# Receiver one-hots 4 and 5 of each ring made on GpSimd instead of VectorE, in a six-convolution graph network on one core

## The reference

```python
edge_index = jnp.stack([src, dst])
h = jnp.maximum(_layernorm(x, axis=-1), 0.0)
x = x + _L0_gnn_ref(h, edge_index, L0_gnn_W_l, L0_gnn_b_l, L0_gnn_W_r)
...
# in each convolution, in one form or another:
summed = jax.ops.segment_sum(x[src], dst, num_segments=n)
deg = jax.ops.segment_sum(jnp.ones_like(src, dtype=x.dtype), dst, num_segments=n)
agg = summed / jnp.maximum(deg, 1.0)[:, None]
out = agg @ W_l.T + b_l + x @ W_r.T
```

## Time and profile before

| | us |
|---|---|
| median of 3 runs (650.18 to 650.49) | 650.31 |
| the profiled execution | 649.73 |
| its span | 647.9 |
| PE busy | 632.0 (98%) |
| DVE busy | 373.8 (58%) |
| ACT busy | 304.1 (47%) |
| POOL busy | 112.5 (17%) |

### The profile page before, as it was taken

How to read it: one execution, slowest core, us unless ns; L and a number is a source line. 1 busy time by engine, 2 the same in 40 slices (tenths; PEclk the granted TensorE clock), 3 DMA queues, 4 the chain that set the end, 5 groups by cost and what they waited for, 6 DMA issues and landing times.

```text
span 647.9 us, 10703 instructions
## 1 busy us (share of the span) xinstructions
PE 632.0 (98%) x3079; PEld 514.0 (79%) x3080; DVE 373.8 (58%) x863; ACT 304.1 (47%) x628; POOL 112.5 (17%) x104
## 2 busy tenths in 40 slices
PE   6989999999999999999999999999999999999997
PEld 4346777777888888888888888888888998899886
DVE  6998999766885333222333787444989730541222
ACT  4886886645334454321223342223678752555210
POOL 2000000000332300321410321430364070000000
PEclk9999999999999999999999999999999999999999
DMA  6311111228450202240201231211200000000102
GB/s 217 114 21 22 31 30 30 42 55 243 122 140 16 49 0 82 61 101 17 49 0 42 57 102 28 45 20 50 82 0 1 2 2 1 0 2 0 50 18 95
DMA packets 57953, 33.04 MB, mean 51 GB/s; under 512 B 45756, under 2 KB 49652, under 8 KB 57912
## 3 DMA queue, kind: packets, MB, share of 16 engines
q1 hardware_dynamic: 56632, 29.99, 18.0%
q10 hardware_dynamic: 1280, 2.56, 1.1%
HBM read 17.20 MB, written 4.20 MB: 33 GB/s over the span
## 4 chain that ended last, share of the span: by engine, by line
PE 91%; DVE 3%; issue 2%; DVEq 1%; DMA 1%; ACT 1%; ACTq 1%; SPq 0%
PE ps L1605 34%; PE ps L1698 27%; PE ps L1737 13%; PE ps L1763 8%; PE ps L1584 7%; DVE src_hot L1119 1%; DMA wstage<-in_L_gnn_W_l 1%; PE ps L1598 1%; PE ps L1546 1%; DVE p_lo L1373 0%; DVE stats L1091 0%; DVEq L1119 0%; DVE dst_hot L1117 0%; DVE own L1333 0%; ACTq L374 0%
## 5 line engine op out<-in xcount | busy, mean ns | idle before, releaser
L1698 PE MATMUL ps<-p_hi,cstage 128*128 128x512 f32 x400 | 156.0, 390 | 0.5 <-ACT cstage L750 0.5
L1698 PE MATMUL ps<-p_lo,cstage 128*128 128x512 f32 x400 | 155.7, 389 | 0.0
L1605 PE MATMUL ps<-w_hi,hT_hi 128*128 128x512 f32 x320 | 126.2, 394 | 0.5 <-issue 0.5
L1605 PE MATMUL ps<-w_hi,hT_lo 128*128 128x512 f32 x320 | 124.6, 389 | 0.0
L1605 PE MATMUL ps<-w_lo,hT_hi 128*128 128x512 f32 x320 | 124.6, 389 | 0.0
L1698 PEld LDWEIGHTS ps<-p_hi,cstage 128*128 128x128 f32 x400 | 75.1, 188 | 16.7 <-issue 0.9
L1698 PEld LDWEIGHTS ps<-p_lo,cstage 128*128 128x128 f32 x400 | 75.1, 188 | 15.5
L1119 DVE TENSOR_SCALAR src_hot<-iota,nodeT 128x640 bf16<-128x640 f16 x210 | 71.0, 381 | 4.0 <-issue 1.7
L1584 PE MATMUL ps<-src_hot,dst_hot 128*128 128x320 bf16 x420 | 67.5, 306 | 5.2 <-DVE src_hot L1119 2.7
L548 POOL COPY halves<-own 128x1024 uint16<-128x1024 uint16 x30 | 33.4, 1113 | 222.2 <-DVE own L1132 191.9
L1605 PEld LDWEIGHTS ps<-w_hi,hT_hi 128*128 128x128 f32 x320 | 60.1, 188 | 13.4 <-issue 1.0
(11 more groups left out here) (156 smaller groups left out, 932.9 us busy)
## 6 DMA issues: line engine op xcount, KB each, us to landing
x<-in_x ACTq DMA_DIRECT2D x1, 2304.0 KB
out_x<-x SPq DMA_DIRECT2D x9, 256.0 KB
wstage<-in_L_gnn_W SPq DMA_DIRECT2D x2, 1024.0 KB, 5.4
swap<-count SPq DMA_DIRECT2D x2, 800.0 KB, 8.6
count<-swap SPq DMA_DIRECT2D x2, 800.0 KB, 8.2
wstage<-in_L_gnn_W_l SPq DMA_DIRECT2D x2, 512.0 KB, 4.1
w_own<-in_L_gnn_W_r SPq DMA_DIRECT2D x1, 1024.0 KB, 11.0
vec<-in_L_gnn_b SPq DMA_DIRECT2D x4, 256.0 KB, 4.8
```

Of the source, the lines that this page charges most:

```text
L1605: last = nc.tensor.matmul(ps[:, bank, :], a[:, r, k, :], w[:, slot, k, :], start=n == 0, stop=n == len(pairs) - 1)
L1698: last = nc.tensor.matmul(ps[:, AGG + r, :], cstage[:, part, k, :], p_[:, k, :], start=n == 1, stop=n == 2 * len(parts) * NT)
```

## The change

GpSimd takes over the dst_hot of slots 4 and 5 in all rings. Per window it loads the window's word (`visits_of`), copies the window's row of `tab` to a fixed place, `tab_now`; per ring it copies the two receiver keys of slots 4 and 5 from `nodeT` to `key_now`, waits for this copy, and then makes each one-hot when its slot is free, with the same compare as VectorE did. A new pair of signals `last_rows[h]` counts them, and TensorE waits for it ahead of slots 4 and 5. VectorE keeps the six src_hot. The two small buffers lie in space of `exact`, which is idle then. The wait of TensorE is the only one added outside of GpSimd.

```diff
+    tab_now, _ = place("tab_now", [P, P], FP16, place.end)
+    key_now, _ = place("key_now", [P, RING - BY_ACT], F32, place.end)
...
+            def last_receivers(b, h):
+
+                n0, n1, offset = visits_of(pool, visited, b, h)
+                nc.gpsimd.tensor_copy(tab_now[:, :].unsqueeze(1), tab[:, window(b, h), :]).then_inc(tab_set, 1)
+                pool.wait_ge(tab_set, 2 * b + h + 1)
+                pool.sem_inc(passed_pool, 1)
+                with pool.Fori(n0, n1, RING) as n:
+                    t = tile_at(pool, n, offset)
+                    nc.gpsimd.tensor_copy(key_now[:, :], nodeT[:, 0, bass.ds(t + BY_ACT, RING - BY_ACT)]
+                                          ).then_inc(key_set[h], RING)
+                    pool.wait_ge(key_set[h], n + RING)
+                    pool.sem_inc(passed_pool, 1)
+                    for e in range(BY_ACT, RING):
+                        pool.wait_ge(hot_used[h], n + e + 1)
+                        nc.gpsimd.tensor_scalar(dst_hot[h][:, e, :], tab_now[:, :], key_now[:, e - BY_ACT:e - BY_ACT + 1],
+                                                None, ALU.is_equal).then_inc(last_rows[h], RING // (RING - BY_ACT))
+                    pool.wait_ge(last_rows[h], n + RING)
+                    pool.sem_inc(passed_pool, 1)
+
+            pool.wait_ge(nodes_placed, 1)
+            pool.wait_ge(table_step, steps_of_table)
+            pool.wait_ge(pool_consts, 4)
+            with pool.Fori(0, NT) as b:
+                for h in range(2):
+                    last_receivers(b, h)
...
                         dve.wait_ge(hot_used[h], n + e + 1)
-                        if e >= BY_ACT:
-                            dve.sem_inc(passed_dve, 1)
-                            nc.vector.tensor_scalar(dst_hot[h][:, e:e + 1, :], tab[:, window(b, h), :],
-                                                    nodeT[:, 0, bass.ds(t + e, 1)], None, ALU.is_equal)
                         nc.vector.tensor_scalar(src_hot[h][:, e, :], iota[:, :], nodeT[:, 1, bass.ds(t + e, 1)], None,
                                                 ALU.is_equal).then_inc(givers_ready[h], 1)
...
                             pe.wait_ge(first_rows[h], n + RING + 3 + 3 * e // 2)
+                        if e >= BY_ACT:
+                            pe.wait_ge(last_rows[h], n + 3 * (e - BY_ACT + 1))
                         pe.wait_ge(givers_ready[h], n + e + 1)
```

More of the change, by code:

```diff
@@ L160, in gnn_kernel @@
     deg_win, _ = place("deg_win", [P, NT, 2], F32, place.end)
+    tab_now, _ = place("tab_now", [P, P], FP16, place.end)
+    key_now, _ = place("key_now", [P, RING - BY_ACT], F32, place.end)
+    assert place.end <= exact_at + P * 4
     feats, u_hi, u_lo = [None, None], [None, None], [None, None]
@@ L215, in gnn_kernel @@
     w_loaded, wT_ready, whi_done, wlo_done = sem("w_loaded"), sem("wT_ready"), sem("whi_done"), sem("wlo_done")
-    givers_ready, hot_used, first_rows, apart_done = (
-        [sem(f"{what}{h}") for h in range(2)] for what in ("givers_ready", "hot_used", "first_rows", "apart_done"))
+    givers_ready, hot_used, first_rows, last_rows, apart_done = (
+        [sem(f"{what}{h}") for h in range(2)]
+        for what in ("givers_ready", "hot_used", "first_rows", "last_rows", "apart_done"))
+    tab_set, key_set = sem("tab_set"), [sem(f"key_set{h}") for h in range(2)]
     nodes_placed = sem("nodes_placed")
@@ L490, in _ @@
                                channel_multiplier=0, allow_small_or_imprecise_dtypes=True).then_inc(pool_consts, 1)
+            visited = [pool.alloc_register(f"pool_visited{h}") for h in range(2)]
+            for h in range(2):
+                pool.reg_mov(visited[h], 0)
+            def last_receivers(b, h):
[19 more added lines that the diff above has]
+            with pool.Fori(0, NT) as b:
+                for h in range(2):
+                    last_receivers(b, h)
             pool.wait_ge(counts_out, NW + 2)
```

## The result

| | us |
|---|---|
| before, median of 6 runs beside the change (649.27 to 650.49) | 649.8 |
| the change, median of 6 runs (654.38 to 656.31) | 655.25 |
| ratio, 95% interval | 1.0081 (1.0071 to 1.0091) |
| the change's profiled span (before: 647.9) | 652.7 |

The change is slower by 0.8%, 5.3 us. The forecast was 648.1 with a range to 651.8, so it is wrong in sign and size.

The account below looks back on a forecast made before the run. VectorE's ring was taken to bound the first 50 us, with TensorE busy 98% overall. Terms -3.84 + 0.2 + 1.4 = -2.24 us took 650.31 to 648.1 us (46%), range 646.4 to 651.8.

Parts of the forecast that it names:

- What bounds the kernel: First 50 us: VectorE's ring of 2.35 us sets the pace, ScalarE's 2.11 is next, TensorE is far behind.
- What goes: VectorE's dst_hot of slots 4 and 5 in the first four windows, 0.16 us each: 3.84 us gained.
- The price of a one-hot, 0.29 us: GpSimd's compare over 128 columns takes 0.29 us, like its select; 0.42 from above by the two-input add.
- Is GpSimd in time: Two one-hots, signals and a wait take 0.9 to 1.0 us of slot 4's 1.36: 0.4 to spare.
- The full stretch: From 50 to 145 us, where TensorE is nearly always busy: no gain and no loss, set at 0.
- The price on VectorE: GpSimd's hold on the shared port costs VectorE 0.20 us per ring: 0.2 and 1.4 us in the first four windows.
- GpSimd is late: Rival, 6%: one-hots over 0.45 us make TensorE wait in rings behind a window's first, +3 to +6 us, about 652.
- VectorE is held off longer than it saves: Rival, 12%: waits at slots 4 and 5 in all 13 rings, then the full stretch, give +2.7 us, 653.0.
- The price eats the gain: Rival, 21%: GpSimd's hold costs VectorE 0.3 to 0.35 us a ring, so the time stays at 650.3.
- The port costs nothing to speak of: Rival, 15%: GpSimd's hold fits into the gaps between VectorE's streams, -3.8 us, 646.5.
- The range: For 8 in 10: 646.4 to 651.8 us, with 0.15 of chance beyond it and 0.05 below.
- The signs of being wrong: Compare over 0.45 us, src_hot's mean from 0.38 to over 0.46 us, or TensorE's busy share from 50 us on falling.

Follow-up runs that it names:

- the masked kernel: The kernel before with one more register operation per window and engine, which masks the window's length: 650.33 us, 1.0008 of before.
- the run without copies: The change without GpSimd's copies of table and keys and its waits for these and the ring's end (wrong one-hots): 650.88 us, 1.0014 of before.
- contention alone: GpSimd makes its one-hots into a place nobody reads, VectorE makes all it made before, TensorE does not wait for GpSimd: 652.88 us, 1.0037 of before.
- the wait alone: What TensorE's wait for GpSimd's pair adds to the run with contention alone: 0.0080 of before, 5.2 us.
- a short one-hot: The change, but GpSimd compares 32 of the 128 columns, the other 96 being zeros: 646.49 us, 0.9952 of before.
- one slot of six: The change, but GpSimd makes slot 5 alone and VectorE slot 4 again: 649.0 us, 0.9981 of before.
- contention and the wait: GpSimd's one-hots go to a place nobody reads, VectorE makes all it made before, TensorE waits for GpSimd's pair: 657.59 us, 1.0117 of before.
- The change with the masked length: The change with one more register operation per window and engine, which masks the window's length: 655.53 us, 1.0086 of before.

## Why the prediction was wrong, step by step

- **What bounds the kernel**: right. With slots 4 and 5 left out, TensorE runs at ScalarE's ring of 2.11 us, as read from the earlier trace rows, and 5.7 us come out.
- **What goes**, 3.84 us: too small by 1.6 to 1.9. I counted 24 dst_hot of the first 13 rings at 0.16 and set the later windows to 0. With the slots left out, the first first_p comes 4.1 us (against the masked kernel) to 4.8 us sooner, and the stretch up to window (5, 0) is 0.7 to 1.0 us shorter. So half or more of the difference is from the full stretch, where TensorE had waited 1.5 us for src_hot as well.
- **The price of a one-hot, 0.29 us**: this step failed. Of three bounds in the earlier trace rows I took the select, as the nearest in shape, and called the two-input add's 2.5 ns a column the far end. The compare runs at 2.4 ns a column with 0.29 us of its own start: 0.60 alone, 0.73 in the kernel. Even my far end, 0.42, was too low, as it took the start of a one-element memset, 0.1, for that of any instruction.
- **Is GpSimd in time**: the test was the right one, with its threshold of 0.45 us for a one-hot, but with the wrong number in it. (It held both one-hots against slot 4's 1.36 us, though slot 5 is wanted 0.27 later. By window (4, 0) of the run without copies two of 0.60 would be just in time in the full stretch, and with VectorE's hold on the first, 1.05 in all, they are late.) It also looked at the two one-hots alone and not at the whole ring: end of the one-hots, loop, keys and wait for the keys are 1.12 us more (0.61 + 0.19 + 0.33, rounded). "The keys are copied before" was false: one place for the keys means that they can't be copied until the last one-hot has read the old ones.
- **The full stretch**: "I set 0" failed with the price of the one-hot. The change takes 48.3 to 49.0 us from the first first_p to window (5, 0) instead of 45.5 to 45.8, which is over half of the loss in either pair of profiles. I asked there only whether VectorE keeps its margin, and not whether GpSimd's pair comes in time.
- **The price on VectorE**: 0.2 a ring for 11 rings, less what gaps take, was 1.6 us; contention alone measured 2.4. The size of a usual meeting (0.07 to 0.1) was right; what was missing is the full stretch, with 1.4 us in the profiled execution. "Neither starves" does not hold in general, by the 3.63 us for two one-hots.
- **The rivals**: "GpSimd is late" is what happened, with its mechanism and its place (slots 4 and 5, rings behind a window's first), and with a part in it for VectorE's hold on GpSimd, which it did not name. I gave it 6% and 652 us, because with 0.29 it could not be; its gross size of +3 to +6 us holds the 5.2 us of the wait alone. "VectorE is held off longer than it saves", 12%, is refuted as the cause: contention costs 2.4 and the relief gives 5.5. The same two numbers speak against "The price eats the gain" and "The port costs nothing to speak of" as far as VectorE alone goes. The Trainium skill's rule that moving work from VectorE to GpSimd might not help since they share a port (Perfetto Trace Analysis, Optimizing Scalar/DVE Operations) is borne out in its cause by the 2.4 us, but with a short one-hot the move wins 3.1 us all the same.
- **The range**: its high end came from cases priced with 0.29 too. One number stood in all of them.
- **The signs of being wrong**: two of the three came. The compare takes 0.73, over 0.45, and TensorE's busy share from the first first_p to window (5, 0) fell from 99% to 97%. The mean of src_hot rose only from 0.38 to 0.39 us.

The account, in shares of the kernel before: relief -0.0084, contention +0.0037, the wait for GpSimd +0.0080, which make +0.0033; measured +0.0081 to +0.0086. The missing 0.005 is the relief that does not come through once GpSimd sets the pace: beside the wait it is worth 0.0031 to 0.0036 and not 0.0084. Each term carries an interval of 0.001 to 0.002.

## What to carry to other kernels

Price an instruction on an engine that has never run it from both of its terms, start and rate, and if no row has its kind, take the slowest rate that the engine shows and see whether the plan stands; a number that all rivals share is no range. When work moves to an idle engine, add up that engine's whole loop, with the copies and waits that it needs for itself, and compare it with the slot's time and with the ring's, before counting what the busy engine gains. Ask this in each stretch by itself, the full one too. A smaller share (one slot of six) can win where the full one loses.

## What the runs showed of the hardware that was not expected

- GpSimd's tensor_scalar costs 2.4 ns a column in float16 and float32, compare or multiplication, on top of 0.29 us, while its copy of 128 columns takes 0.29 in all. The Trainium skill (GPSIMD Engine Reference, When to use GPSIMD) calls one-input elementwise operations on this engine roughly line-rate. The copies come to 0.8 ns a column (1.04 us for 1024 less 0.29 for 128, an estimate across two types), and the tensor_scalar takes three times that, which speaks against the sentence.
- In one execution TensorE's granted clock fell behind the wait of 1.46 us that ended at 41.35, by windows of the kernel after (us, PE busy, PEld, DVE, ACT, POOL, PEclk, DMA):

```profile
41.00:42.80 1.80, 1.27 (x7) 0.54 (x8) 0.81 (x4) 1.80 (x8) 0.99 (x3) 1.00 0.15 32
43.00:46.00 3.00, 3.00 (x14) 2.03 (x13) 2.57 (x8) 1.33 (x5) 1.60 (x3) 0.50 0.11 21
```

  That is 1.2 GHz in place of 2.4. Whether the wait brought it on is not shown: in the kernel with contention and the wait TensorE stood 1.79 us ahead of 33.86, and its granted clock stayed at 1.00 from 33 to 51 us. The change with the masked length had no such fall either (granted clock 1.00 over its span) and took as long, so it is not the cause of the loss.
- Executions differ at the start of the counting. In the profiled execution of before 72 matmuls took 14.33 us from 13.54, the first 16 of them 0.27 us apart and not 0.136. That is the step of the stretch at 0.50 above, though the profile gives the granted clock as 1.00 here. In that of the same kernel with the masked length the first 12 took the normal time:

```profile
13.91 1.80 PE L1584 MATMUL ps<-src_hot,dst_hot 128*128 128x320 bf16 x12 [1.88 <-ACT dst_hot L714]
```

  The change goes the other way: normal steps in its profiled execution, the first 10 or so 0.27 us apart in that with the masked length. So it does not go with the mask. Before and its masked form are 0.6 us apart at the next window (28.6 against 29.2 us), likely for this reason, so the verdicts above go by the ratios.
